# Four selective-scan setups of a four-layer network rearranged: operands by halves of the sequence, VectorE alone for sums and products, table loads ahead, convolution apart from the copies

## The reference, cut to what matters

```python
xm, z = jnp.split(h @ W_in, 2, axis=-1)            # 512 channels each
xm = silu(causal_depthwise_conv4(xm) + conv_b)     # u
dtr, Bm, Cm = jnp.split(xm @ W_xp, [64, 80], axis=-1)
dt = jax.nn.softplus(dtr @ W_dt + b_dt)            # delta
A = -jnp.exp(A_log)                                # 512 x 16
h_t = h_{t-1} * exp(dt_t * A) + (dt_t * u_t) * B_t # 16 states for each channel
y_t = sum_s h_t * C_t + u_t * D
y = y * silu(z)
return y @ W_out
```

## Time and profile before

| | us |
|---|---|
| median of 3 runs (2214.99 to 2222.23) | 2215.05 |
| profiled execution, its own time | 2217.42 |
| span of the profiled execution | 2215.7 |
| TensorE busy | 2018.9 (91%) |
| VectorE busy | 1613.1 (73%) |
| ScalarE busy | 1438.8 (65%) |
| GpSimd busy | 1061.2 (48%) |

### The profile page before, as it was taken

How to read it: one execution, slowest core, us unless ns; L and a number is a source line. 1 busy time by engine, 2 the same in 40 slices (tenths; PEclk the granted TensorE clock), 3 DMA queues, 4 the chain that set the end, 5 groups by cost and what they waited for, 6 DMA issues and landing times.

```text
span 2215.7 us, 34737 instructions
## 1 busy us (share of the span) xinstructions
PE 2018.9 (91%) x13528; PEld 1417.9 (64%) x13528; DVE 1613.1 (73%) x2067; ACT 1438.8 (65%) x2422; POOL 1061.2 (48%) x594
## 2 busy tenths in 40 slices
PE   6969799887998899989999999899988999998997
PEld 4844699737997499759984899599842222332333
DVE  5554699447996499769984899599768777776621
ACT  3314799347983699589845997799642655554564
POOL 1021499405994199639950799299624100111000
PEclk9989799987999899999999999999998999998998
DMA  4040111101111011102100111111101111111000
GB/s 175 1 141 20 43 58 58 41 13 55 58 57 50 20 54 58 35 23 55 54 24 2 49 58 49 35 54 58 29 22 38 30 29 30 29 28 30 9 20 20
DMA packets 54161, 95.04 MB, mean 43 GB/s; under 512 B 11815, under 2 KB 20167, under 8 KB 52590
## 3 DMA queue, kind: packets, MB, share of 16 engines
q1 hardware_dynamic: 52462, 88.63, 13.2%
q0 software_dynamic: 1536, 4.20, 0.6%
HBM read 73.29 MB, written 6.91 MB: 36 GB/s over the span
## 4 chain that ended last, share of the span: by engine, by line
PE 66%; POOL 8%; ACT 8%; DVE 8%; issue 8%; DMA 1%; SPq 0%; POOLq 0%; DVEq 0%; ACTq 0%
PE PS L723 11%; PE PS L745 11%; POOL A L857 7%; PE PS L1408 6%; PE PS L253 5%; PE PS L1360 5%; PE PS L1546 5%; PE PS L728 5%; PE PS L244 4%; PE PS L608 2%; PE PS L751 2%; ACT A L809 2%; PE PS L1090 1%; DVE A L1029 1%; DVE A L1373 1%
## 5 line engine op out<-in xcount | busy, mean ns | idle before, releaser
L857 POOL TENSOR_TENSOR A<-A 128x1024 f32<-128x1024 f32 x384 | 897.9, 2391 | 138.1 <-ACT small L798 126.1
L809 ACT ACTIVATE A<-A,negA 128x512 f32<-128x512 f32 x768 | 546.6, 712 | 42.5 <-DVE A L842 32.9
L842 DVE TENSOR_TENSOR_SCAN A<-A,PS 128x512 f32<-128x512 f32 x384 | 434.4, 1199 | 55.0 <-ACT A L809 36.3
L842 DVE TENSOR_TENSOR_SCAN A<-A,small,PS 128x512 f32<-128x512 f32 x384 | 455.2, 1256 | 6.1 <-PE PS L723 5.5
L745 PE MATMUL PS<-ident,A 128*128 128x128 f32 x3072 | 401.3, 273 | 18.8 <-POOL A L857 13.8
L1582 ACT ACTIVATE A<-PS 128x1024 f32<-128x1024 f32 x256 | 262.2, 1024 | 222.0 <-PE PS L1546 220.4
L723 PE MATMUL PS<-A 128*128 128x128 f32 x3072 | 392.4, 280 | 5.6 <-DVE A L842 5.6
L1373 DVE TENSOR_REDUCE A<-PS 128x1 f32<-128x512 f32 x512 | 329.8, 686 | 80.7 <-PE PS L1360 77.3
L723 PEld LDWEIGHTS PS<-A 128*128 128x128 f32 x3072 | 371.5, 196 | 14.2 <-DVE A L842 7.8
L745 PEld LDWEIGHTS PS<-ident,A 128*128 128x128 f32 x3072 | 346.6, 141 | 28.8 <-POOL A L857 19.0
L783 ACT ACTIVATE A<-A,small 128x512 f32<-128x512 f32 x340 | 239.9, 710 | 24.3 <-PE PS L728 20.2
(11 more groups left out here) (198 smaller groups left out, 2045.5 us busy)
## 6 DMA issues: line engine op xcount, KB each, us to landing
A<-scrc SPq DMA_DIRECT2D x192, 256.0 KB, 3.1
A<-A SPq DMA_DIRECT2D x360, 32.0 KB
scr<-A SPq DMA_DIRECT2D x4, 1024.0 KB, 4.6
W<-in_wa SPq DMA_DIRECT2D x2, 1536.0 KB, 10.1
X<-in_x SPq DMA_DIRECT2D x4, 512.0 KB, 5.4
out<-X SPq DMA_DIRECT2D x2, 1024.0 KB, 4.5
W<-in_w SPq DMA_DIRECT2D x1, 1984.0 KB, 8.3
W<-in_wzc SPq DMA_DIRECT2D x1, 1536.0 KB, 11.8
```

The source lines that it names most:

```text
L809: e.activation(A_B[i % 4], r.DT[:, dt, ci * 512:(ci + 1) * 512], ACT.Exp, scale=negA[:, r.n, dt * 16 + s:dt * 16 + s + 1]).then_inc(*decay ...
L842: e.tensor_tensor_scan(h, a, u, init, ALU.mult, ALU.add).then_inc(*scanned.up((q, i)))
L857: e.tensor_tensor(h, h, CB[k % 2].unsqueeze(1).broadcast_to([128, 2, 512]), ALU.mult).then_inc(*weighed.up((q, pair)))
```

## The change

Delta and delta times u are made by halves of the sequence, all groups of a half at once, in the order in which the scan takes the halves. VectorE makes all sums and products; GpSimd's instruction is gone. DUD is laid out by halves, and the two halves' transposes take banks 4 to 7 and 0 to 3 (seek). A small Exp on a spare column is put ahead of the Abs instructions and again behind the Ln instructions. ScalarE makes the first four decays and a diagonal of B before it copies the turned product, of which the second half's copies stand behind the first scaling by B, and in runs 0 and 1 fuse_s has moved in there too. The wait for C's store is now in front of the decays; scan loads of C wait for the first product alone. The buffers H are rotated by one, so that the first pair doesn't lie over DUD. In the Mamba layer the eight copies of xm come first, then the four Silu with the z tiles spread between them, and the padding is zeroed by VectorE. The additions to the residual (lines 1034 and 1151) stand ahead of the sums. z_t and z_s go by halves.

```diff
-        DUD = area(29712, 4, S)
+        DUD = area(29712, 2, 4, 512)
+        spare = small[:, 200:201]
...
-                self.H = [area(WK + 3072 + 1024 * j, 2, 512) for j in range(4)] + [more[1][:, 0:1024]...]
+                self.H = [more[1][:, 0:1024]...] + [area(WK + 3072 + 1024 * j, 2, 512) for j in range(4)]
...
         def inputs_t(e, w, r, ready, meanwhile=None):
-            for c in range(2):
-                ready()
+            for c in r.order:
+                ready(c)
                 project_t(e, w, ("xd", q, c), ...)
-            w.wait_ge(*act.at(("xd", q, 1)))
-            for m in range(4):
-                for c in range(2):
+            for c in r.order:
+                w.wait_ge(*act.at(("xd", q, c)))
+                for m in range(4):
                     o = take(w, ("dt", q, m, c))
...
-            for n in range(2):
-                w.wait_ge(*dve.at(("du", q, n)))
-                for i in range(0, TB, 2):
-                    o = take(w, ("dut", q, n, i))
-                    for j in range(4):
-                        t = e.transpose(o[...], DUD[:, 2 * n + j % 2, ...], ident[:, :])
+            for p, c in enumerate(r.order):
+                banks.seek(0 if p else 4)
+                w.wait_ge(*dve.at(("du", q, p)))
+                for j in range(4):
+                    o = take(w, ("dut", q, p, j))
+                    for m in range(4):
+                        t = e.transpose(o[...], DUD[:, p, m, j * 128:(j + 1) * 128], ident[:, :])
...
         def inputs_s(e, w, r, meanwhile=None):
-            w.wait_ge(*transfer(f"c_store{q}").at(0))
-            for m in range(4):
-                for c in range(2):
+            preload_exp(e, w)
+            for p, c in enumerate(r.order):
+                for m in range(4):
                     w.wait_ge(*pe.at(("dt", q, m, c)))
-                    e.activation(DU[:, m, c * 512:(c + 1) * 512], ..., ACT.Abs, ...)
+                    e.activation(DUD[:, p, m, :], ..., ACT.Abs, ...)
+                w.wait_ge(*act.now())
+                e.activation(DUD[:, p, :, :], DUD[:, p, :, :], ACT.Exp, scale=-1.0).then_inc(*act.up(("exp", q, p)))
             (the two copies of B, as before)
-            (two Exp, two Ln of groups 0-1 and 2-3)
+            for p in range(2):
+                w.wait_ge(*act.at(("exp", q, p)))
+                e.activation(DUD[:, p, :, :], DUD[:, p, :, :], ACT.Ln, bias=1.0).then_inc(*act.up(("ln", q, p)))
             if meanwhile:
                 meanwhile()
-            (six copies of the turned product)
+            preload_exp(e, w)
+
+        def preload_exp(e, w):
+            w.wait_ge(*act.now())
+            e.activation(spare, ones[:, 0:1], ACT.Exp).then_inc(*act.up())
...
         def inputs_v(e, w, r, meanwhile=None, after=None):
+            for p, c in enumerate(r.order):
+                o = slice(c * 512, (c + 1) * 512)
+                w.wait_ge(*dve.at(("relu", q, c)))
+                w.wait_ge(*act.at(("ln", q, p)))
+                e.tensor_tensor(r.DT[:, :, o], r.DT[:, :, o], DUD[:, p, :, :], ALU.add).then_inc(*dve.up(("delta", q, p)))
+                w.wait_ge(*dve.at(("delta", q, p)))
+                e.tensor_tensor(DUD[:, p, :, :], r.DT[:, :, o], r.U[:, :, o], ALU.mult).then_inc(*dve.up(("du", q, p)))
+            if after:
+                after()
+            for j in range(2):
+                w.wait_ge(*pe.at(("dut", q, 1, j)))
+                e.tensor_copy(r.DUT[:, 4 * r.order[1] + j, :], bank(("dut", q, 1, j)))...
-        def inputs_p(e, w, r):
-            e.tensor_tensor(r.DT[:, 2:4, :], r.DT[:, 2:4, :], DUD[:, 2:4, :], ALU.add).then_inc(*pool.up(("dt23", r.q)))
...
         def run_sp(e, w, r):
             w.wait_ge(*transfer(f"c_store{q}").at(0))
-            run_ready(w, r)
+            w.wait_ge(*dve.at(("du", q, 0)))
...
         def run_t(e, w, r, before=None):
-            run_ready(w, r)
+            w.wait_ge(*act.at(("dut", q, 0, 3)))
...
         def run_s(e, w, r, meanwhile=None):
-            for j in range(4):
-                scale_b(0, j)
-            for j in range(4):
-                spread_b(1, j)
+            w.wait_ge(*transfer(f"c_store{q}").at(0))
+            w.wait_ge(*dve.at("neg_a"))
+            for i in range(4):
+                decay(i)
+            for j in range(4):
+                spread_b(1, j)
+            if meanwhile:
+                meanwhile()
+            for j in range(4):
+                copy_du_s(e, w, r, 0, j)
+            for j in range(4):
+                w.wait_ge(*act.at(("dut", q, 0, j)))
+                scale_b(0, j)
+            for j in range(2, 4):
+                copy_du_s(e, w, r, 1, j)
...
         def layer1_sp(e, w):
-            w.wait_ge(*pe.at(("dut", 1, 1, 6)))
+            w.wait_ge(*pe.at(("dut", 1, 1, 3)))
             e.dma_start(W2[:, 0:2816], T["w2"][:, 0:2816])...
             run_sp(e, w, runs[1])
...
         def layer1_p(e, w):
-                e.memset(XM[:, :, 0:3], 0.0).then_inc(*pool.up(("pad", b)))
-                inputs_p(e, w, runs[b])
...
         def layer1_s(e, w):
+                for m, gates in enumerate(((), (0, 1), (2,), (3, 4, 5, 6, 7))):
                     w.wait_ge(*dve.at(("conv", b, m)))
                     e.activation(r.U[:, m, :], ACC[:, m, :], ACT.Silu, ...)
-                for i in range(TB):
-                    w.wait_ge(*pe.at(("z", b, i)))
-                    e.activation(YT1[:, i, :], bank(("z", b, i)), ACT.Silu)...
-                inputs_s(e, w, r, lambda: fuse_s(e, w, b))
-                run_s(e, w, r)
+                    for i in gates:
+                        w.wait_ge(*pe.at(("z", b, i)))
+                        e.activation(YT1[:, i, :], bank(("z", b, i)), ACT.Silu)...
+                inputs_s(e, w, r)
+                run_s(e, w, r, lambda: fuse_s(e, w, b))
...
         def layer1_v(e, w):
-                w.wait_ge(*pool.at(("pad", b)))
+                if b:
+                    w.wait_ge(*pe.at(("yg", 0, 6)))
+                w.wait_ge(*dve.now())
+                w.wait_ge(*transfer("store1_1").at(0))
+                e.memset(XM[:, :, 0:3], 0.0).then_inc(*dve.up())
...
         def z_t(e, w, b, n):          # z_s alike
-            for m in range(4):
-                for c in range(2):
+            for c in runs[2 + n].order:
+                for m in range(4):
```

More of the change, by code:

```diff
@@ L581, in __init__ @@
                 self.wxp, self.wdt, self.bdt, self.dcol = wxp, wdt, bdt, dcol
-                self.H = [area(WK + 3072 + 1024 * j, 2, 512) for j in range(4)] + [more[1][:, 0:1024].rearrange("p (a b) -> p a b", a=2)]
+                self.H = [more[1][:, 0:1024].rearrange("p (a b) -> p a b", a=2)] + [area(WK + 3072 + 1024 * j, 2, 512) for j in range(4)]
                 self.G = [more[0][:, 512 * j:512 * (j + 1)] for j in range(4)] + [more[1][:, 1024:1536], more[1][:, 1536:2048]]
@@ L648, in inputs_s @@
             if meanwhile:
                 meanwhile()
-            for n in range(2):
-                for i in range(0, TB, 2):
-                    if not by_vector(n, i):
-                        w.wait_ge(*pe.at(("dut", q, n, i)))
-                        e.activation(r.DUT[:, i:i + 2, n * 256:(n + 1) * 256], pair(("dut", q, n, i)), ACT.Copy).then_inc(*act.up(("dut", q)))
-                        banks.give(("dut", q, n, i), act.now())
-        def inputs_v(e, w, r, meanwhile=None):
-            q, DU = r.q, DUD
+            preload_exp(e, w)
@@ new lines, in preload_exp, with copy_du_s, inputs_v @@
+        def preload_exp(e, w):
+            w.wait_ge(*act.now())
+            e.activation(spare, ones[:, 0:1], ACT.Exp).then_inc(*act.up())
+        def copy_du_s(e, w, r, p, j):
+            w.wait_ge(*pe.at(("dut", r.q, p, j)))
+            e.activation(r.DUT[:, 4 * r.order[p] + j, :], bank(("dut", r.q, p, j)), ACT.Copy).then_inc(*act.up(("dut", r.q, p, j)))
+            banks.give(("dut", r.q, p, j), act.now())
+        def inputs_v(e, w, r, meanwhile=None, after=None):
+            q = r.q
@@ L692, in store_c_sp, with second_half @@
+            if after:
+                after()
+            for j in range(2):
+                w.wait_ge(*pe.at(("dut", q, 1, j)))
+                e.tensor_copy(r.DUT[:, 4 * r.order[1] + j, :], bank(("dut", q, 1, j))).then_inc(*dve.up(("dut", q, 1, j)))
+                banks.give(("dut", q, 1, j), dve.now())
+        def second_half(w, r):
+            w.wait_ge(*act.at(("dut", r.q, 1, 3)))
+            w.wait_ge(*dve.at(("dut", r.q, 1, 1)))
         def store_c_sp(e, w, r):
-            w.wait_ge(*act.at(("xd", r.q, 1)))
+            w.wait_ge(*act.at(("xd", r.q, r.order[1])))
@@ L707, in run_t @@
             q = r.q
-            for mark in banks.rest():
-                w.wait_ge(*mark)
-            run_ready(w, r)
-            late, opened = [], set()
+            w.wait_ge(*act.at(("dut", q, 0, 3)))
+            opened = set()
             def form_u(i):
@@ L716, in form_u @@
                     ci = r.steps[k][0]
```

(15 more changed lines are left out.)

87 lines of the change are left out of this document (32 added, 55 removed).

## The result

The changed kernel takes 2148.44 us (median of 4 runs, 2145.81 to 2150.57), the kernel before 2216.49 on the same chip (4 runs, 2214.99 to 2222.23). The ratio is 0.9686, 95% interval 0.9663 to 0.9709. The sum had said 2159. Of the two profiled executions, the span went from 2215.7 to 2144.1 us: 71.6 gained where 56.3 were expected. By the medians it is 68, as the profiled execution of the changed kernel (2145.81) is the fastest of four, of which two took over 2150.

A forecast was written before the change was run, and what follows sets the result against it. Four engines are nearly full inside scans, so gains were expected only in setups and Mamba inputs: 7.1 + 16.1 + 24.4 + 6.5 + 4.4 − 2.2 = 56.3 us off 2217.42 gives 2161.1, as a median 2159; range 2143 to 2178.

The forecast's parts named there:

- The sum: Whole kernel: the parts' gains add to 56.3 us, a median of 2159, own range 2150 to 2168, chance 50%.
- The convolution: Mamba input: copies first and earlier padding start the projection sooner, by 7.1 us in element 0, 16.1 in element 1.
- Setups of runs 0 and 1: From ScalarE's second projection copy to the first scan: 28.2 us instead of 40.4, a gain of 12.2 each.
- ScalarE is the last: Setups of runs 0 and 1: ScalarE's scaling ends at 239.8, TensorE's second transposes at 239.2 at worst.
- An early one costs what a late one does: Table loads in the setups: 1.30 us early or late, unless ScalarE is idle there, which it no longer is.
- Runs 2 and 4: Setups: earlier input and a shorter ScalarE chain to the scan gain 6.5 us in run 2, 4.4 in run 4.
- Runs 3 and 5: Setups: the chain behind the last gate grows to 10.9 us, so each scan starts about 1.1 later, −2.2 together.
- rival (a): Setups and scans: no slow-clock spell (5.6 us) and GpSimd's lead passed on (12.6): 2141, or about 2150 with one; 22%.
- The scans: Inside the six scans: taken as 0, with bounds per run of 2.1 us gained and 2.5 lost.
- I take 0, as TensorE is full afterwards: Inside the scans: GpSimd's earlier first product and TensorE's smaller lead both meet at a full TensorE, so nothing changes.
- signs of being wrong: Convolution passes over 1.4 us, an extra table load, GpSimd's first product after 5.5 us, TensorE at half clock beyond 10 us.
- Rival (b): Scan starts: TensorE, cold and without its two-unit lead, holds them, 2.5 us in each of six: 2174 to 2178; 22%.

The follow-up runs named there:

- experiment 12: Kernel before with only the new convolution order of the Mamba input, scan setups unchanged: 2195.49 us, ratio to before 0.9906.
- Experiment 3: Changed kernel with the last of the convolution's four taps left out: 2150.27 us, span 2148.5.
- experiment 7: Changed kernel with the second half's sum back on GpSimd and VectorE's product waiting for it: span 2147.9 us against 2144.1.
- experiment 6: Changed kernel with the halves joined again, so that the scan waits for both: span 2155.0 us against 2144.1.
- experiment 8: Changed kernel without the small Exp instructions that load the table early: span 2144.9 us against 2144.1.
- experiment 5: Changed kernel with one decay made ahead of the copies instead of four: span 2144.9 us against 2144.1.
- experiment 2: Changed kernel with the 1408 KB weight load moved behind the first two C rows of run 1: span 2139.2 us against 2144.1.
- experiment 9: Changed kernel with dt again waiting for both copies of the projection, a pause of 0.68 us: span 2147.5 us against 2144.1.
- experiment 1: Changed kernel with the Mamba input in its old order and the padding zeroed on GpSimd again: 2169.12 us, ratio to before 0.9786.
- experiment 11: Kernel before with only dt, its Abs and its maximum made by halves, each waiting for its own half: 2202.25 us, ratio to before 0.9928.

## Why the prediction was right, and where it was off

**The convolution** (7.1 and 16.1; measured 7.4 and 15.2, by experiment 12 7.2 and 16.4). The size was right, the mechanism half so, and that the size came out is luck. The prediction let VectorE set the end of the input, with the projection near 195. Experiment 3 shows that TensorE does: z takes 13.9 us behind xm, and the projection starts at 197.5. So it starts 4.6 us earlier than before in run 0, and 12.3 earlier in run 1, counted from the end of the scan ahead of it, for the 7.1 and 16.1 expected. The other 2.9 in each come from a term that the sum didn't have: the projection takes 7.03 instead of 9.88 and 9.95. The gathers cost VectorE nothing, as taken.

**Setups of runs 0 and 1** (12.2 each; measured 13.4 and 13.8). "ScalarE is the last" is the step that was off: in run 0 it is TensorE's second half of the transposes, cold; in run 1, where they're warm (1.97), it is the scaling. The first scans came 27.0 and 26.6 after the second copy for the 28.2 expected: the sum of ScalarE's durations was 1.2 too long, as instructions behind one another overlap by some 0.1 (four Abs take 2.41 where 2.53 was used). The sums on VectorE are worth 3.1 and 3.5 of it (experiment 7), the halves 3.8 and 2.3 (experiment 6).

**"An early one costs what a late one does"** failed in runs 0 and 1, where experiment 8 lost 1.3 and 2.2 from the copy without it: the wait for dt and for delta, taken for nothing, is where the load hides. In runs 2 to 5 the sentence holds.

**Runs 2 and 4** (6.5 and 4.4; measured 5.8 and 5.9). Close. From the copy the gains are 5.7 and 3.7, for the 5.6 and 3.5 of the sum. Run 2's missing 0.7 and run 4's extra 1.5 lie ahead of that, mostly in the clock of 32 transposes behind the last scan: in run 2 they took 5.35 us before (at 685.11) and 6.45 now (at 635.46), in run 4 6.62 before (at 1140.36) and 5.35 now (at 1077.15). The change doesn't touch them.

**Runs 3 and 5** (−1.1 each). Run 5 gave −1.15; experiment 5 shows the cause, the 1.8 that three more decays cost. Run 3 gave +5.5, the largest miss of the sum: without the spell of the earlier trace rows its setup would have been 44.3, and 45.5 is the same −1.15 from there. This is the first half of rival (a), which put the spell at 5.6, though its own rows differ by 6.4; it measured 6.6. Both profiles of before have the spell; whether its other executions do isn't known.

**The scans** (0; measured 4.5 in all, with run 1's −1.3). GpSimd's first product came 4.0 us after the first scan, 1.5 earlier than before and not the 2.1 expected, and 1.15 of the 1.5 is passed on; experiment 5 shows that the decays in hand do it. "I take 0, as TensorE is full afterwards" was wrong. The C row behind the weights cost run 1 the 2.4 that experiment 2 takes away, a little more than the "up to 2". Run 1 also showed two of the signs of being wrong: GpSimd's first product came 6.26 us after the first scan, later than the 5.5 named, and TensorE was at half clock 9.1 to 12.5 us into the scan, beyond the 10 named. Rival (b)'s cold TensorE is real (3.65 at 912.38), but it was there before too (3.57 at 972.36), and the scans that begin with it, runs 3 and 5, are 1.15 shorter like the others.

So the median of 2148.44 lies below the sum's own 2150 to 2168, and nearest to rival (a) with one of its two gains, about 2150. It is inside the whole range because (a) was counted in. For the profiled pair: the sum's 56.3, plus 6.6 for the spell, 4.5 from the scans, 2.8 for the setups of runs 0 and 1, and 1.4 of small terms, is 71.6.

## What to carry to other kernels

Before a part is costed against a row, ask whether the stage of that row was disturbed: two setups with the same work, 50.9 and 44.5 us, differed by more than most edits give. Before an edit is read from one profiled span, take off what lies outside it: in experiments 7 and 8 a shorter stretch behind run 5 hid 2.6 and 2.7 us. When a chain is rebuilt, list every engine's end of it, not the last one of before: in the input TensorE took the place that the sum gave to VectorE, 3.3 us behind it, and in run 0's setup the place that it gave to ScalarE, 0.7 behind it. A first use of a buffer that a DMA fills (the C row) should stand ahead of any large transfer on the same queue.

## What the runs showed of the hardware

**A stretch at 1.2 GHz amid full work.** In the dt product of some setups TensorE's granted clock fell to 0.50 for 13.7 us, while it was busy 6.00 of each 6 us; it had been idle for 0.68 us just ahead of the product, and busy for 2.5 to 2.7 us between that and the fall. It was in run 3 in both profiles of before, in run 5 in one of them, in run 2 in the one profile with the input 20 us shorter, and in none of the eleven profiles in which dt goes by halves. It cost 6.6 us in runs 3 and 5 and 3.9 in run 2. Idling 0.68 us doesn't by itself bring it on (experiment 9). The Trainium skill, "TensorE: Matmul & The Clock Gate", "HAM oscillation — how this bites in real kernels", puts the falls of the clock in a matmul kernel down to its waits for DMAs between groups of matmuls. No such wait stands here: a gap of 0.68 stood ahead of every spell, and of the nine setups of before that had none. What brings it on stays open: the form of dt and the phase at which the setup falls were not separated.

**The same idle time, different clocks.** After an idle time of 3.29 to 3.30 us the projection of the Mamba layer took 9.88, 9.95, 10.06 and 10.05 us in the two profiles of before, 8.73 and 10.07 in experiment 1, 8.55 and 7.08 in experiment 11. Without the idle time it took 7.03 in every profile.

**Gathers beside the convolution.** GpSimd's indirect DMA instructions took 0.95 us alone and 1.01 to 1.68 in batch element 1, where VectorE's passes ran beside them (1.68 at 423.50), while the passes kept their 1.3.
